# Turning the routed experts' inner rows: by the DMA engines' transposes in place of TensorE's

## The reference, cut to what matters

```
def expert_step(acc, ws):
    gw, uw, dw, ce = ws                       # [512, 352], [512, 352], [352, 512], weight per token
    out = silu(x @ gw) * (x @ uw) @ dw
    return acc + ce[:, None] * out, None
moe_out, _ = scan(expert_step, zeros_like(x), (gate_w, up_w, down_w, combine.T))
```

## Time and profile before

| | |
|---|---|
| median of 3 runs | 1762.69 us (1761.22 to 1765.13) |
| the profiled execution's own time | 1761.46 us |
| its span, first to last instruction | 1759.6 us |
| PE busy | 1572.1 us (89%) |
| DVE, ACT, POOL busy | 1091.7, 756.3, 512.9 us |
| mean granted TensorE clock | 0.954 of full speed |
| expert phase, first expansion to last contraction | 486.45 to 730.30 us |

### The profile page before, as it was taken

One profiled execution on the slowest core, in us unless ns is written; L12 is line 12 of the kernel. 1 busy time (PEld: TensorE's weight loads), 2 busy tenths in 40 slices (PEclk: granted clock), 3 DMA queues, 4 the chain that ended last, 5 costly groups with the idle time before them and its releaser, 6 DMA issues. The chain is left out here.

```text
span 1759.6 us, 27544 instructions
## 1 busy us (share of the span) xinstructions
PE 1572.1 (89%) x9484; PEld 913.1 (52%) x9484; DVE 1091.7 (62%) x2221; ACT 756.3 (43%) x1392; POOL 512.9 (29%) x428
## 2 busy tenths in 40 slices
PE   4989948999799999879888887889999999999997
PEld 3778833444356566435344443545555555555554
DVE  7998845335623343368586874766676767575663
ACT  5443214333123333234343452656564656566462
POOL 0657824333324444234342331120202010111101
PEclk7999979999999999889899998989999999999998
DMA  9545544745596898552425226624160505142241
GB/s 208 140 118 155 161 143 137 202 145 154 169 213 177 220 221 198 206 197 84 144 84 168 66 77 239 199 61 92 41 132 6 125 18 113 41 90 60 61 91 42
DMA packets 293579, 228.83 MB, mean 130 GB/s; under 512 B 197778, under 2 KB 241298, under 8 KB 291170
## 3 DMA queue, kind: packets, MB, share of 16 engines
q1 hardware_dynamic: 244912, 156.73, 34.7%
q10 hardware_dynamic: 39298, 40.54, 7.9%
q0 software_dynamic: 9264, 30.15, 5.6%
HBM read 125.58 MB, written 54.87 MB: 103 GB/s over the span
## 5 line engine op out<-in xcount | busy, mean ns | idle before, releaser
L2136 POOL TENSOR_TENSOR s_h_lo<-s_h,s_h_hi 128x512 f16<-128x512 f32 x32 | 36.9, 1154 | 552.8 <-DVE s_h_hi L2338 552.8
L1275 DVE TENSOR_TENSOR e_h<-e_up,e_silu 128x352 f32<-128x352 f32 x39 | 20.4, 524 | 138.7 <-ACT e_silu L1220 123.5
L2356 PE MATMUL s_ring<-w_mu,s_xt_hi 128*128 128x512 f16 x256 | 98.5, 385 | 5.9 <-DMA w_mu<-mu_split 2.8
L2264 DVE TENSOR_REDUCE s_top<-s_lg 128x1 f32<-128x512 f32 x64 | 43.9, 686 | 93.4 <-ACT s_lg L2178 93.2
L2357 PE MATMUL s_ring<-w_mu,s_xt_hi 128*128 128x512 f16 x256 | 98.5, 385 | 0.0
L2358 PE MATMUL s_ring<-w_mu,s_xt_lo 128*128 128x512 f16 x256 | 98.2, 384 | 0.0
L2356 PE MATMUL s_acc<-w_w,s_g_hi 128*128 128x512 f16 x256 | 97.1, 379 | 0.1
L524 PE MATMUL ring<-prod_hi,toep 128*128 128x288 f16 x320 | 92.8, 290 | 4.9 <-DVE terms L438 4.7
L2356 PE MATMUL s_ring<-w_w,s_xt_hi 128*128 128x512 f16 x256 | 97.0, 379 | 0.0
L2357 PE MATMUL s_ring<-w_w,s_xt_hi 128*128 128x512 f16 x256 | 97.0, 379 | 0.0
L2358 PE MATMUL s_ring<-w_w,s_xt_lo 128*128 128x512 f16 x256 | 97.0, 379 | 0.0
(11 more groups left out here) (387 smaller groups left out, 4793.7 us busy)
## 6 DMA issues: line engine op xcount, KB each, us to landing
expert_rows<-e_y SPq DMA_DIRECT2D x39, 256.0 KB
a_part_in<-in_L_ffn_W ACTq DMA_DIRECT2D x32, 256.0 KB
w_split<-a_part_q ACTq DMA_DIRECT2D x32, 256.0 KB
w_w<-w_split SPq DMA_DIRECT2D x8, 1024.0 KB, 21.6
toep<-ssm_split ACTq DMA_DIRECT2D x14, 512.0 KB, 5.3
stage<-in_L_ffn_gate_w SPq DMA_DIRECT2D x8, 704.0 KB
stage<-in_L_ffn_up_w SPq DMA_DIRECT2D x8, 704.0 KB
xattn_w_split<-e_part_q ACTq DMA_DIRECT2D x20, 256.0 KB
```

Source lines behind the costliest of these rows:

```text
L2264: V.tensor_reduce(top[:, t, j:j + 1], lg[:, t, j * D:(j + 1) * D], AX.X, ALU.max).then_inc(S["top_done"], 1)
L2356: mm(out_, a[0], b_[0], start=first, stop=False)
```

## The change

The hi and lo halves of h are made while h still lies with the tokens on the partitions, in SBUF, and are then turned together by one DMA transpose. ACT makes hi (one copy of 128x352) right behind the Silu of the same tile, DVE makes lo (one subtraction) right behind its product, both into `e_hq`, 2 x 384 columns of fp16 a row; the last 32 columns of each half are cleared once at the start. SP turns tile n-3 in iteration n, behind the transpose of `e_xt` and ahead of the output store: 6 blocks of 128x128, 192 KB, into `e_ht`. `e_silu` and `e_h` shrink to one buffer each. The PE transposes, the PSUM bank `e_h_turn` and the four copies out of it go.

```diff
-        h_hi, h_lo = sb("e_h_hi", [P, U, MK, P], F16), sb("e_h_lo", [P, U, MK, P], F16)
+        hq, ht = sb("e_hq", [P, U, 2, MK * P], F16), sb("e_ht", [P, U, 2 * MK, P], F16)
...
+            for u in range(U):
+                nc.gpsimd.memset(hq[:, u, :, I_MOE:MK * P], 0.0).then_inc(edge_cleared, 1)
...
-                if early >= 2 and late <= 2:
-                    u = (r - 2) % U
-                    pe.wait_ge(h_done, n - 1)
-                    if early >= 3:
-
-                        pe.wait_ge(h_lo_done, (n - 2) * 2)
-                    for q in range(MK):
-                        i_ = slice(q * P, min((q + 1) * P, I_MOE))
-                        last = nc.tensor.transpose(h_turn[0:i_.stop - i_.start, q, :], h[:, u, i_], k.ident[:, :])
-                    last.then_inc(h_turned, 1)
...
-                    pe.wait_ge(h_lo_done, (n - 2) * 2)
+                    pe.wait_ge(h_turned[u], ((n - 3) // U + 1) * 16)
...
-                    nc.scalar.activation(silu[:, (r - 1) % U, :], gate_ps[:, (r - 1) % 2, 0:I_MOE], ACT.Silu).then_inc(silu_done, 1)
-                if early >= 2 and late <= 2:
-                    act.wait_ge(h_turned, n - 1)
-                    if early >= 5:
-
-                        act.wait_ge(contracted, n - 4)
-                    for rows_, blocks in parts:
-                        nc.scalar.activation(h_hi[rows_, (r - 2) % U, blocks, :], h_turn[rows_, blocks, :], ACT.Copy).then_inc(h_hi_done, 1)
+                    nc.scalar.activation(silu[:, :], gate_ps[:, (r - 1) % 2, 0:I_MOE], ACT.Silu).then_inc(silu_done, 1)
+                    if n > U:
+
+                        act.wait_ge(h_turned[(n - 1) % U], (n - 1) // U * 16)
+                    act.wait_ge(h_done, n)
+                    nc.scalar.activation(hq[:, (r - 1) % U, 0, 0:I_MOE], h[:, :], ACT.Copy).then_inc(h_hi_done, 1)
...
-                    if early >= 4:
-
-                        dve.wait_ge(h_turned, n - 3)
-                    nc.vector.tensor_tensor(h[:, (r - 1) % U, :], up_ps[:, (r - 1) % 2, 0:I_MOE], silu[:, (r - 1) % U, :],
+                    if early >= 2:
+                        dve.wait_ge(h_lo_done, n - 1)
+                    nc.vector.tensor_tensor(h[:, :], up_ps[:, (r - 1) % 2, 0:I_MOE], silu[:, :],
                                             ALU.mult).then_inc(h_done, 1)
-                if early >= 2 and late <= 2:
-                    dve.wait_ge(h_hi_done, (n - 1) * 2)
-                    for rows_, blocks in parts:
-                        nc.vector.tensor_tensor(h_lo[rows_, (r - 2) % U, blocks, :], h_turn[rows_, blocks, :],
-                                                h_hi[rows_, (r - 2) % U, blocks, :], ALU.subtract).then_inc(h_lo_done, 1)
+                    dve.wait_ge(h_hi_done, n)
+                    nc.vector.tensor_tensor(hq[:, (r - 1) % U, 1, 0:I_MOE], h[:, :], hq[:, (r - 1) % U, 0, 0:I_MOE],
+                                            ALU.subtract).then_inc(h_lo_done, 1)
...
+            def turn_h(n):
+                u = n % U
+                if n < U:
+                    sp.wait_ge(edge_cleared, n + 1)
+                else:
+                    sp.wait_ge(contracted, n - U + 1)
+                sp.wait_ge(h_lo_done, n + 1)
+                sp.dma_start_transpose(ht[:, u], hq[:, u].rearrange("p q i -> p (q i)")).then_inc(h_turned[u], 16)
+
...
                 sp.dma_start_transpose(xt[:, u], rows[:, u, :]).then_inc(turned[u], 16)
+                if n >= 3:
+                    turn_h(n - 3)
                 if n >= LAG:
                     store(n - LAG)
                 background(n)
+            for n in range(TILES - 3, TILES):
+                turn_h(n)
+                store(n - LAG + 3)
```

More of the change, by code:

```diff
@@ L1051, in expert_phase @@
     assert TILES % U == 0
-    MT = MK - 1
-    TAIL = I_MOE - MT * P
     with phase(nc) as st:
@@ L1060, in expert_phase @@
         ones = sb("e_ones", [P, 1])
-        silu, h = sb("e_silu", [P, U, I_MOE]), sb("e_h", [P, U, I_MOE])
-        h_hi, h_lo = sb("e_h_hi", [P, U, MK, P], F16), sb("e_h_lo", [P, U, MK, P], F16)
+        silu, h = sb("e_silu", [P, I_MOE]), sb("e_h", [P, I_MOE])
+        hq, ht = sb("e_hq", [P, U, 2, MK * P], F16), sb("e_ht", [P, U, 2 * MK, P], F16)
         y = sb("e_y", [P, U, D])
@@ L1067, in expert_phase @@
         part_hi, part_lo = sem("e_part_hi"), sem("e_part_lo")
-        mu_ps, h_turn = ps("mu_ps", [P, D]), ps("e_h_turn", [P, MK, P])
+        mu_ps = ps("mu_ps", [P, D])
         gate_ps, up_ps, out_ps = ps("e_gate", [P, 2, D]), ps("e_up", [P, 2, D]), ps("e_out", [P, 2, D])
@@ L1077, in expert_phase @@
         expanded, silu_done, h_done = sem("e_expanded"), sem("e_silu_done"), sem("e_h_done")
-        h_turned, h_hi_done, h_lo_done = sem("e_h_turned"), sem("e_h_hi_done"), sem("e_h_lo_done")
+        h_hi_done, h_lo_done, edge_cleared = sem("e_h_hi_done"), sem("e_h_lo_done"), sem("e_edge_cleared")
+        h_turned = [sem(f"e_h_turned{u}") for u in range(U)]
         contracted, y_done = sem("e_contracted"), sem("e_y_done")
@@ L1172, in step @@
                         n_ = min(P, I_MOE - q * P)
-                        a_hi, a_lo = (a[0:n_, u, q, :] for a in (h_hi, h_lo))
+                        a_hi, a_lo = (ht[0:n_, u, part * MK + q, :] for part in range(2))
                         w_hi, w_lo = (a[0:n_, bass.ds(expert, 1), q, :].rearrange("p o d -> p (o d)") for a in (w.down_hi, w.down_lo))
@@ L1195, in _ @@
             over_tiles(step, background)
-        parts = ((slice(0, P), slice(0, MT)), (slice(0, TAIL), slice(MT, MK)))
         @block.scalar
@@ L1343, in _ @@
                 background(n)
+            for n in range(TILES - 3, TILES):
+                turn_h(n)
+                store(n - LAG + 3)
             for n in range(TILES, FIRST + PERIOD * (NJ - 1) + 13 + KD):
                 background(n)
-            for n in range(TILES - LAG, TILES):
+            for n in range(TILES - LAG + 3, TILES):
                 store(n)
```

## The result

The changed kernel takes 1767.76 us in the median of 12 runs (1764.52 to 1773.72), the kernel before 1762.04 (1756.61 to 1765.59) in the runs beside it. The ratio is 1.0037, 95% interval 1.0023 to 1.0051: 4 to 9 us slower. The forecast was 11 us less. The measured time lies outside the range, on the side that had a chance of 0.15. The profiled execution took 1773.72 us, the slowest of the 12, so its gaps may be larger than those of the others.

What follows compares the result with a forecast made beforehand. PE's own work was taken to bound the expert phase. Transposes -12.9, the gap at 602 us +1.0 and the end +0.2 gave -11.7 us: 1751.0 us for the median (1749.8 for the profiled execution), range 1745 to 1766.

Steps and rivals of the forecast that it cites:

- PE's transposes: On PE between expansion and contraction: 39 tiles x 0.33 us leave PE's path, 12.9 us saved.
- The gap at 602 us: PE's stall behind the last mu load: load some 2 us later, stall stays 2.9 us; +1.0 us, bounds -4.6 and +4.
- SP: One more DMA issue per iteration, 0.93 us for 6 blocks; the output store slips by less than 1 us.
- The chain to the contraction: Expansion end to turned h: issue at +2.3 us, landing 4.5 or 7.7, spare 4.2 or 1.0; wait normally met early.
- The DMA sum: Whole expert phase: plain traffic plus turns of rows and h take 194 us, under the 231 us PE would need.
- The lower price: DMA transfer of one turn of h at 201 GB/s: 1.0 us, 194 us for the phase; the price taken.
- the upper price: DMA transfer at 147 GB/s: 1.35 us per turn of h; with share read as fill, 248 us, more than PE needs.
- The rival of dense stretches: Iterations 17 to 20 and 24 to 27: eight tiles lose 0.7 us each, 5.6 us, giving 1757; chance 0.20.
- the DMA becomes the bound: Rival over the whole phase: the DMA queue needs 248 us against PE's 231, +10 us, giving 1772; chance 0.13.
- ACT and DVE: One copy on ACT (hi, 0.46 us), one subtraction on DVE (lo, 0.5, bound 1.9); no cost by themselves.
- The end: After the last expansion, PE waits for the last turn of h: +0.2 us, bounds 0 and +3.
- theory B: From the experiments, not the prediction: turns of h cost wherever they are, because the DMA is full through the phase.

Runs made afterwards that it cites:

- e17: Kernel before, without the eight mu loads of quarters 2 and 3, 1 MB context load in four pieces at iterations 10 to 16: 0.9961 of the kernel before.
- e18: Changed kernel without turns of h (PE takes unturned halves), without the eight late mu loads, 1 MB load in four pieces: 0.991 of the kernel before.
- e1: Changed kernel without its DMA turns of h; PE contracts with the unturned halves: 0.994 of the kernel before, 10.6 us faster.
- e16: Changed kernel without the eight late mu loads, 1 MB context load in four pieces at iterations 10 to 16: 0.9914 of the kernel before.
- e4: Changed kernel with ACT's squares of mu two steps later and POOL's sums one step later, same DMA traffic: 0.9996 of the kernel before.
- e5: Changed kernel with ACT's mu squares two steps later, POOL's sums one later, 1 MB load in four pieces: 0.995 of the kernel before.
- e3: Changed kernel with the 1 MB load of context rows issued at iteration 11 instead of 19: 1.003 of the kernel before.
- e7: Changed kernel turning only the hi half (3 blocks instead of 6), which PE also takes for lo: 0.999 of the kernel before.
- e9: Changed kernel with the turn of h ahead of the row turn in SP's iteration: 1.0059 of the kernel before.
- e11: Changed kernel with 1 MB load in four pieces, mu squares one step later, turn of h ahead of the row turn: 0.9979 of the kernel before.
- e12: Kernel before with the 1 MB load in four pieces and ACT's mu squares one step later, POOL's sums unmoved: 0.997 of the kernel before.
- e10: Changed kernel with the 1 MB load in four pieces and ACT's mu squares one step later, POOL's sums unmoved: 0.9974 of the kernel before.
- the last runs: Both kernels without the eight late mu loads, with the 1 MB load whole or in four pieces, once without turns: 0.991 to 0.9961 of the kernel before.
- e6: Kernel before with ACT's mu squares two steps later, POOL's sums one later, 1 MB load in four pieces: 0.9977 of the kernel before.

## Why the prediction was wrong

**PE's transposes: right.** Between e17 and e18, which for PE differ by the transposes alone and have no gap in between, the phase is 237.2 - 224.3 = 12.9 us shorter, the 39 x 0.33 of the text. In the kernel as it is, e1 gave 10.6 us (to about 4 us), in which ACT's wait for mu grew to 12.7 us in its profiled execution and PE stood 5.2 us behind it.

**The gap at 602 us: this is the step that failed.** It took the mu load to come 2 us later, and the stall to stay at 2.9 us; +1.0 us, bounds -4.6 and +4. In the profile ACT's wait is 16.7 us instead of some 11, there is a second gap of 4.8 us at 659 to 664 us, and PE's waits of all kinds are 20.7 us against 3.4, so +17.3 us. The phase grew by 12.7 us; with 12.9 us saved the gaps and what they did to the clock are 25.6 us, of which 8.3, by difference, belong to the clock. By the medians it is less: 17 us between e1 and the changed kernel.

Two things in this term were wrong. The smaller is the distance of the load from PE. The text reckoned from the end of an expansion, at 590.9, and took the load to keep its distance to it but for one more issue and transfer. Counted from the first expansion, in the profiled executions:

| us from the first expansion | before | e1, no turns | with the change |
|---|---|---|---|
| expansion ends; ACT does its Silu, then waits for mu | 104.5 | 99.9 | 98.6 |
| last mu load issued | 108.7 | 107.5 | 109.8 |
| ACT goes on | 114.8 | 114.4 | 117.1 |

Rid of its transposes, PE is there 5.9 us sooner; the load is not. Behind the end of the expansion ACT goes on after 18.5 us instead of 10.3, where the text had some 12.3. In e1, without a single turn of h, it is already 14.5: half of the extra distance comes without the turns, and there too one row turn's issue holds SP for 6 us. Its lines:

```profile
586.49 6.03 SPq L1335 DMA_TRANSPOSE e_xt<-e_rows  x1
...
593.81 0.63 SPq L1300 DMA_DIRECT2D mu_in<-in_L_ffn_mu  x1
...
600.80 2.19 ACT L1235 ACTIVATE mu_square<-mu_in 128x512 f32<-128x512 f32 x4 [12.74 <-DMA mu_in<-in_L_ffn_mu]
```

The turns' own share of the landing, 114.4 to 117.1, is 2.7 us, close to the "some 2 us" of the text. The larger mistake is PE's wait for turned rows. PE's waits behind late mu loads grew only from 3.4 to 6.9 us; those for turned rows took 11.9 us before the last tile, where this term had up to 1 us for one tile and the chain below none. They come from SP's backlog and from its wait for lo.

**SP: the issue was mis-sized.** 0.93 us by blocks; it is 1.21 at the least, and 3.12 behind the stuck row turn. That row turn, the first issue behind the 1 MB load, holds SP for 6.57 us, where the longest of these before was 2.69. The text had "it slips by less than 1 us".

**The chain to the contraction: right in light stretches, not in dense ones.** In e16 the turns of h land after 2.7, 3.6 and 7.7 us (least, median, most), inside the 4.5 and 7.7 that were used. In the changed kernel the row turns take up to 11.3 us to land against 7.7, and PE waited for turned rows 8 times. The 1.0 us that the text left "at worst" was the reserve on which all hung, and it took the issue to follow lo at once: the turn of 595.81 left 6.0 us after its lo, and then took 8.3 us. Where ACT stands, lo itself is late.

**The DMA sum: right, as far as it went.** The lower price was taken because the stretch with share 1.08 had no gap; e16 shows 200 us at 1.04 without one, so the share is not a fill level. By the upper price e16 would have needed 0.78 x 237.2 us (share and phase of e17) and 53 us of turns, 238 us; its phase took 226.4. As a mean over the phase that says nothing about 1 MB and eight turns in one place. The rival of dense stretches had the place right and its price, 0.7 us a tile, far too low; "the DMA becomes the bound" had nearly the size, and a cause, turns dear everywhere, that e16 and e18 speak against. The 175 us that the text gave for transposes as fast as regular transfers leaves the row turns at 1.3 us each; with these at 0.68 us too it would be 150. Nothing hung on it, and the trace's 201 against 386 GB/s stands against that speed; no run measured it again.

**ACT and DVE.** hi takes 0.50 us, lo 0.53 in the median, as reckoned (0.46 and 0.5). ACT stands 36.6 us for DVE's products; in e16 it stands 25.8 us for them, and PE has no gap in 200 us. Three lo took 2.94 to 3.34 us beside POOL's work, more than the bound of 1.9.

**The end.** +0.2 was reckoned. PE stands 1.89 us for the last turn, as in e16, where the 2.1 us of phase between it and e18 are the whole cost of the turns. The next phase then starts 5.3 us behind the last contraction instead of 4.0, which the sum didn't have.

What stays open: why some issues of a transpose hold SP for 3 to 6 us, why the first block of the turn costs as much as it does (0.004), and whether the late loads or the load in one lump carries more of the loss. e4 and e5 suggest about 7 and 8 us for them in this order, but e3, the lump moved alone, gave 1 us, so they don't add. With the late loads in place theory B's figures came out in e3, e7, e9, e11 and for e12 against e10; what the last runs refute is only that a turn costs wherever it is. That SP, ACT and PE wait for each other in a ring is seen in the profile; what the ring costs, and that each link is needed, was not tried.

## What to carry to other kernels

A DMA that fits by bytes into the mean of a phase still has to fit in its densest place: look there for the load that an engine waits for in line, and count the whole backlog before it, not one transfer. When a bound engine gets faster, it comes to such a load sooner, and the load need not: e1 alone shows half of the extra distance. An in-order issuer that is given a wait on a compute engine joins that engine to every other transfer in its queue, as from 603.4 to 611.6 here. Before work moves from a bound engine to the DMA, pull back the consumers of late loads and break up the lump, and measure both kernels so: in e5 and e6 the same two edits made the loss of 6 us a gain of 5 over its own control, with one step less (e10, e12) a gain of nothing, each to about 4 us. The Trainium skill, DMA: Bandwidth & Descriptors, section Rules for kernel authors, says to issue a DMA early and wait for it late; e4, two steps later, was worth 7 us, so the runs agree.

## What the runs showed of the hardware

- The issue of a transpose on SP depends little on its size: medians of 1.13 us for 1 block, 1.20 for 3, 1.26 for 6 and 1.30 for 8 (row turns of the changed kernel).
- The same issue can hold SP much longer than its median: 6.57 us right behind a load of 1 MB, and 6.03 in e1, one row turn further on, against 1.24 at the least. Before the change the same two places took 1.76 and 2.69 us.
- A busy share above 1 can be held for 200 us (1.04 at 245 GB/s, e16) without a gap on PE.
- A subtraction on DVE of 128x512 that takes 0.68 us took 4.62 us where POOL worked beside it (changed kernel, 612.07).
